# Attention worked off in pairs of units with the next sample's projections inside the drain, and a first graph layer from a 42-node operand

## What is computed

```python
# 1. tokens: 3 graph-attention layers on 4 x 128 graphs of 50 nodes, 3 -> 64 -> 128 -> 64 channels
for W, a_s, a_d, bg, R, g, b in layers:          # first layer: x has 3 channels
    h = _gat(x, src, dst, W, a_s, a_d, bg)       # softmax over the edges of a node, 4 heads
    res = x @ R
    x = gelu(_layer_norm(h + res, g, b))
h = _layer_norm(x.reshape(Bb * Tt, J * 64) @ fpW + fpb)
h = concatenate([h, text_rows_gathered_from_a_table], axis=1)      # 4 x 640 x 128
# 2. four state-space layers (scan over 640 positions, 256 channels x 64 states)
h = h + _L0_attn_ref(_layernorm(h), ...)
# 3. attention that keeps the 16 largest logits of each row, 8 heads of 16 channels
x = _layernorm(h);  x = x + depthwise_conv3(x)
q, k, v = split(x @ qkv_w.T + qkv_b)
_, idx = lax.top_k(q @ k.T * scale, 16)
out = softmax over idx, times v;  h = h + out @ wo_w.T + wo_b
```

## Time and profile before

| | |
|---|---|
| median of 3 runs | 6161.43 us (6158.26 to 6162.38) |
| the profiled execution | 6194.43 us, of which 6192.4 us are the span in the trace |
| embed_stage | 0 to about 1220 us |
| mamba_stage | about 1220 to 5400 us |
| ffn_stage | about 5400 us to the end |
| DVE busy | 5546.6 us, 90% of the span |
| PE busy | 3863.3 us, 62% |

### The profile page before, as it was taken

One profiled execution on the slowest core, in us unless ns is written; L12 is line 12 of the kernel. 1 busy time (PEld: TensorE's weight loads), 2 busy tenths in 40 slices (PEclk: granted clock), 3 DMA queues, 4 the chain that ended last, 5 costly groups with the idle time before them and its releaser, 6 DMA issues. The chain is left out here.

```text
span 6192.4 us, 60179 instructions
## 1 busy us (share of the span) xinstructions
PE 3863.3 (62%) x13720; PEld 2225.0 (36%) x13720; DVE 5546.6 (90%) x7803; ACT 3290.5 (53%) x5742; POOL 4510.6 (73%) x3041
## 2 busy tenths in 40 slices
PE   3402432237767677677676776766767766577767
PEld 3202421123334333333333333433333333265556
DVE  3798678839999999999999999999999999787778
ACT  1302232226666666666666666666666665554445
POOL 3303210329999999999999999999999999633334
PEclk9756576659999999999999999999999999888788
DMA  1000000024444444444444444444444444200000
GB/s 28 1 11 1 2 1 11 1 90 173 170 170 168 171 168 170 168 172 169 169 170 168 168 172 169 168 169 168 170 169 171 166 168 169 100 2 2 2 2 2
DMA packets 171471, 694.85 MB, mean 112 GB/s; under 512 B 27969, under 2 KB 34626, under 8 KB 171138
## 3 DMA queue, kind: packets, MB, share of 16 engines
q1 hardware_dynamic: 169608, 688.25, 30.7%
q0 software_dynamic: 1536, 3.14, 0.2%
HBM read 684.77 MB, written 6.55 MB: 112 GB/s over the span
## 5 line engine op out<-in xcount | busy, mean ns | idle before, releaser
L851 POOL TENSOR_TENSOR m_hs<-m_u,m_BC 128x1280 f32<-128x1280 f32 x1024 | 2990.4, 2920 | 76.5 <-DVE m_u L1232 76.5
L1198 DVE TENSOR_TENSOR_SCAN m_hs<-m_PS,m_hs 128x640 f32<-128x640 f32 x2048 | 2964.0, 1476 | 12.6 <-ACT m_PS L908 6.7
L1082 PE MATMUL m_PS<-m_pr,ident 128*128 128x512 f32 (+1 forms) x6144 | 2443.4, 534 | 846.5 <-DVE m_pr L1206 846.1
L1082 PEld LDWEIGHTS m_PS<-m_pr,ident 128*128 128x128 f32 x6144 | 1110.8, 191 | 2079.0 <-DVE m_pr L1206 1077.6
L908 ACT ACTIVATE m_PS<-m_dt,m_A 128x640 f32<-128x640 f32 x2048 | 1612.4, 793 | 430.5 <-DVE m_hs L1198 404.4
L858 POOL TENSOR_TENSOR m_pr<-m_hs,m_BC 128x384 f32<-128x384 f32 x1024 | 1047.5, 1023 | 95.2 <-DVE m_hs L1198 93.4
L1206 DVE TENSOR_TENSOR m_pr<-m_hs,m_PS 128x896 f32<-128x896 f32 x1024 | 1087.4, 1062 | 7.2 <-DVE m_hs L1198 6.9
L292 POOL TENSOR_TENSOR g_prod<-g_hbuf,g_E 128x128 f32<-128x128 f32 x592 | 246.1, 452 | 862.8 <-ACT g_E L344 845.6
L897 ACT COPY m_PS<-m_BC 128x448 f32<-128x448 f32 x1024 | 548.2, 535 | 427.0 <-DVE m_u L1232 83.1
L1416 POOL TENSOR_SCALAR f_negm<-f_top 128x1 f32<-128x1 f32 x160 | 33.5, 209 | 449.4 <-DVE f_top L1616 278.0
L378 PE MATMUL g_TB<-ident,g_nrm 128*128 128x128 f32 x200 | 64.3, 323 | 440.2 <-DVE g_nrm L517 429.2
(11 more groups left out here) (246 smaller groups left out, 4486.6 us busy)
## 6 DMA issues: line engine op xcount, KB each, us to landing
m_BC<-m_scr SPq DMA_DIRECT2D x1024, 640.0 KB, 3.7
m_scr<-m_CB SPq DMA_DIRECT2D x32, 160.0 KB, 4.3
m_hs<-in_cwr SPq DMA_DIRECT2D x4, 512.0 KB, 3.9
out<-f_res SPq DMA_DIRECT2D x20, 64.0 KB, 1.6
m_inw<-in_in_w SPq DMA_DIRECT2D x4, 256.0 KB, 3.9
m_dtw<-in_dw SPq DMA_DIRECT2D x4, 256.0 KB, 3.6
m_xw<-in_xw SPq DMA_DIRECT2D x8, 64.0 KB, 3.7
m_outw<-in_ow SPq DMA_DIRECT2D x4, 128.0 KB, 3.4
```

The costliest lines, as they stand in the source:

```text
L851: pool.tensor_tensor(hs[:, g % RH], u[:, p % 2], BC[:, g % UB:g % UB + 1, 0:S].to_broadcast([P, DT, S]), ALU.mult).then_inc(w_ready, 1)
L1082: ins = pe.matmul(Y[:, a:e], ident[:], pr[:, g % RP, a:e], start=False, stop=False, skip_group_check=True)
L1198: v.tensor_tensor_scan(hs[:, g % RH, d, :], half[d], hs[:, g % RH, d, :], 0.0, ALU.mult, ALU.add).then_inc(scan_done, 1)
```

## The change

Four things change.

1. **Start.** SP issues the edge loads first, then the 8 loads that the first layer needs, then the ids; it no longer waits for the clears ahead of the edge loads. The other 26 loads go out on ACT's queue. POOL makes its index rows ahead of the clears. DVE waits for the edges alone, then for the 8 first loads (the score columns of layer 0 now stand ahead of the sorted edges), and for the other 26 only ahead of layers 1 and 2.
2. **First layer.** `wc[0]` is loaded with each of its 3 rows repeated 42 times (126 rows). ACT makes 42 blocks from it, each masked to the three rows of one node (`block0`, 126 x 136 each), which live in the buffer `accB`. The coordinates of 42 nodes at a time are the stationary operand (126 rows), and one matmul of 272 columns does a group of two nodes. PE waits for all 42 blocks. For the second pair of samples the blocks are made, and the coordinates loaded, during layer 2 of the first pair.
3. **Pairs.** The attention works off units two at a time. DVE runs each of its four steps for both units before the next step; `e_all`, `negm` and `top1` have four buffers instead of two, `cut1` two instead of one. PE, ACT and POOL follow in pairs.
4. **Drain.** The loop over the samples is written out. The preparation of the next sample is cut into four steps, which stand between the last pairs of the sample before it, on every engine.

The core of the diff:

```diff
+                for dst, at in loads_first():
+                    sp.dma_start(dst, at).then_inc(first_loaded, 16)
                 sp.wait_ge(cleared, 3)
...
+                rest = loads_rest()
+                for dst, at in rest:
+                    act.dma_start(dst, at).then_inc(loaded, 16)
+                act.wait_ge(wc0_ready, 1)
+                def blocks():
+                    for j in range(CH):
+                        act.activation(block0[:, j, :], wc[0][:], ACT.Copy, scale=mask[:, j:j + 1]).then_inc(block_ready, 1)
+                blocks()
...
+                            if l == 0:
+                                k = 0 if 2 * g < CH else 1
+                                at = 2 * g - CAT[k]
+                                pe.matmul(banks(l, G).rearrange("p a n -> p (a n)"), x0C[:, bb, k, :],
+                                          block0[:, at:at + 2, :].rearrange("p a n -> p (a n)"),
+                                          start=True, stop=True).then_inc(proj_ready, 1)
...
                     if pb:
-                        sp.wait_ge(nrm_ready, pb * (3 * NG))
+                        sp.wait_ge(nrm_ready, (pb * 3 - 1) * NG)
...
-                    for c in range(UNITS + 5):
-                        if c + 1 < UNITS:
-                            logits(c + 1)
-                        if 2 <= c < UNITS + 2:
-                            transposes(c - 2)
-                        if 3 <= c < UNITS + 3:
-                            pv(c - 3)
+                    for n in range(LONG):
+                        if n >= PER + 3 and (n - PER - 3) % PER == 0:
+                            o_out((n - PER - 3) // PER, 1)
+                        old = 2 * (n - 2)
+                        if 2 <= n < PAIRS + 2:
+                            transposes(old)
+                            transposes(old + 1)
+                            pv(old)
+                        if n + 1 < PAIRS:
+                            logits(2 * n + 2)
+                            logits(2 * n + 3)
+                        if 2 <= n < PAIRS + 2:
+                            pv(old + 1)
+                        if n >= PER + 2 and (n - PER - 2) % PER == 0:
+                            o_out((n - PER - 2) // PER, 0)
+                        if b + 1 < B and 0 <= n - PAIRS < 4:
+                            prepare(b + 1, n - PAIRS)
```

More of the change, by code:

```diff
@@ L264, in _ @@
                 pool.memset(ones[:], 1.0).then_inc(iota_ready, 1)
+                pool.memset(ids[:], 4 * VOCAB).then_inc(cleared, 1)
+                pool.memset(x_tok[:], 0.0).then_inc(cleared, 1)
+                pool.memset(after[:], 0.0).then_inc(cleared, 1)
                 pool.wait_ge(cleared, 3)
@@ L433, in chain, with scores @@
                     v.wait_ge(setup, done[0])
[L435 to L438 removed]
+                def scores(l, k):
+                    n = COUT[l]
+                    for s in range(2):
+                        chain(v.tensor_tensor(awork[0:k, 0:n], wc[l][:, 0:n], avec[0:k, l, s, 0:n], ALU.mult))
+                        chain(v.tensor_reduce(wc[l][:, 2 * n + s * H:2 * n + (s + 1) * H],
+                                              awork[0:k, 0:n].rearrange("p (h c) -> p h c", h=H), AX.X, ALU.add))
+                v.wait_ge(edges_loaded, 3 * 16)
                 v.wait_ge(iota_ready, 4)
@@ L1395, in _ @@
                 pool.tensor_scalar(tap1[:], taps[:, 1:2], 1.0, None, ALU.add).then_inc(pre_pool, 1)
-                with pool.Fori(0, B) as b:
+                for b in range(B):
                     pool.wait_ge(pre_dve, b * N_DVE + 1)
@@ new lines, in prepare @@
+                def prepare(b, step):
+                    if step == 1:
+                        pe.wait_ge(pre_dve, b * N_DVE + 6)
+                        if b:
+                            pe.wait_ge(cut1_ready, b * UNITS)
+                            pe.wait_ge(exp_ready, b * UNITS)
+                        for j in range(TILES):
+                            ins = pe.transpose(LGf[:, j * P:(j + 1) * P], xn[:, j, :], ident[:])
+                        ins.then_inc(pre_pe, 1)
+                    elif step == 2:
+                        pe.wait_ge(pre_dve, b * N_DVE + 9)
+                        proj(LGf, 0, wq[:]).then_inc(pre_pe, 1)
+                        if b:
+                            pe.wait_ge(probT_copied, b * UNITS)
+                        proj(PT, 0, wk[:]).then_inc(pre_pe, 1)
+                    elif step == 3:
+                        pe.wait_ge(pre_dve, b * N_DVE + 10)
+                        for j in range(TILES):
+                            ins = pe.matmul(LGf[:, j * P:(j + 1) * P], x2[:, j * P:(j + 1) * P], wv[:],
+                                            start=True, stop=True)
+                        ins.then_inc(pre_pe, 1)
@@ L1492, in logits @@
+                for step in range(4):
+                    prepare(0, step)
+                for b in range(B):
                     def logits(c):
@@ L1592, in finish_a @@
+                for step in range(4):
+                    prepare(0, step)
+                for b in range(B):
+                    g0 = b * UNITS
                     def finish_a(t):
```

369 lines of the change are left out of this document (204 added, 165 removed).

## The result

The changed kernel takes 6057.22 us (median of 4 runs, 6031.34 to 6077.31), the kernel before 6160.3 (4 runs too). That is 103 us by the medians. The ratio is 0.9828, with a 95% interval of 0.9801 to 0.9856, which makes 106 us, or 1.7%, faster. The forecast was 6073. The profiled execution took 6077.31 us, of which 6075.6 are the span; it stands 20 above the median.

A forecast was written before the change was run, and what follows sets the result against it. Bound: TensorE at half clock in the first layer, DVE waiting for its own results in the attention. Gains 29 + 25 + 0 + 24 + 10 = 88; 6194.4 - 88 = 6106, less 33.0 (profiled execution above median): 6073; range 5965 to 6150.

The forecast's parts named there:

- start: Ahead of the first layer: TensorE starts at 48 in place of 77, a gain of 29 us.
- first pass: First layer, first two samples, during the gathers: gain counted as 0, ends a loss of 21 and a gain of 21.
- second pass: First layer, second two samples: full clock and no wait for coordinates, a gain of 25 us, 0 as other end.
- gaps between samples: Attention, last replacing to next first maximum: 31 us in place of 39.0, a gain of 3 x 8 = 24.
- pairs: Attention, two units at a time: 7.75 us a pair in place of 7.88, a gain of 10 us over 80 pairs.
- formula for T: Attention, pair time from share s at half clock: T = 1/((1 - s)/6.8 + s/12.1), 7.75 us at s = 0.28.
- B: Rival, attention: the clock holds in pairs, 6.95 us a pair at s = 0.05, total 6009 us; chance 0.25.
- C: Rival, attention: interleaving gains nothing on DVE, the pair stays at 7.88 us, total 6083 us; chance 0.04.
- D: Rival, first layer: the 126-row operand doesn't lift the clock, second pass wins only 4.5, total 6093 us; chance 0.08.
- F: Rival, start: blocks or edge loads come at the slow pace, TensorE starts at 74, total 6099 us; chance 0.08.
- E: Rival, attention: TensorE at half clock most of the time, 9.5 us a pair at s = 0.65, total 6213; chance 0.10.

The follow-up runs named there:

- three-row run: The changed kernel with 3 of the 126 rows of the first layer's stationary operand kept, so its results are not the model's: 6109.49 us (one run).
- unit-by-unit orders: The changed kernel with TensorE going transposes, logits, product for each unit: 6564.07 us; the same with ScalarE's exp ahead of its `PT` copy: 6202.67 us.

## Why the prediction was right, point by point

The time, 6057 beside a forecast of 6073, lay in the range, and the direction held. Step by step it was less good: errors cancel, and that the sum came within 16 us is luck.

| term | forecast | measured |
|---|---|---|
| start | 29 | 17.4 (45.7 against the profiled execution) |
| first pass | 0 | 20.3 |
| second pass | 25 | 27.0 |
| gaps between samples | 24 | -1.8 |
| pairs | 10 | 27.8 |
| end of the kernel | not counted | -9.6 |

The terms sum to 81 of 106. The profiled execution of the changed kernel, from which they are read, stands 20 above its median; that the other runs had a faster pattern of the attention is likely but was not profiled. Some 5 are left, about what the middle stage differs by from trace to trace.

- **Start.** The step that failed is "The chain from L458 (36.73) to TensorE's start takes 40.7 us", taken as a property of the kernel: in the two other traces of this embed_stage it takes 12.2 and 11.8. The profiled execution stood 33.0 above the median; 28 of these were that very chain's slow pace, and I used them twice, in the chain and in the 33.0 taken off at the end. L458 itself was put at 13 and came at 16.34. I forecast that the chain ends last. It ended at 27.01, and what ended last were the blocks: their 12.65 us were right (12 to 13), but they begin at 18.94, behind 26 DMA issues on the same queue and a table load.
- **First pass.** "I count 0" was the middle of two ends. Measured is the upper end, 20.3 (25.4 us of projections in place of 45.7). On the chip with the slow pace the pass took 69.2 and 69.6 us, a loss of 24, a little beyond the lower end.
- **Second pass.** Right: 23.2 us measured, 24.5 forecast, no wait, and the blocks (473 to 486) hidden in layer 2. The three-row run shows that it is the rows.
- **Gap.** "I take 31 for the gap" failed. The mechanism (transposes and projections queued behind the drain on TensorE) was named but not worked out: at half clock four units' products and transposes take until 5896.7. The sum started from the gap of before, whose drain had one or two units left, where pairs leave four. Against pairs without the drain it saves 6.7 a gap, close to the 8 that I took. The end of the kernel has the same longer drain without anything to hide it: from the last replacing 22.3 us in place of 12.8, a term that was missing.
- **Pairs.** In the fast samples (granted clock 0.94) 135.6/20 = 6.78, forecast 6.8 at full clock, and TensorE became the bound. The wait for the copy is 0.87, forecast 1.11. Slow pairs take up to 11.7, forecast 12.1. The granted clock over the samples (0.78, 0.74, 0.94, 0.94) weighted by the samples' times, is a share of 0.32 at half clock, forecast 0.28. The formula for T put 7.75, and would put 7.9 at 0.32; measured is 603.1/80 = 7.54. So the share was somewhat worse than forecast and the time better, since the formula charged too much for it. The reason given for the share was "it was in stretches without logits that the clock fell". The trace of the kernel before does not bear it out (14 of 19 falls within a sample came while logits ran), and the unit-by-unit orders speak against it. That the number was near is luck.
- **Rivals.** B (the clock holds) is what samples 3 and 4 show; C falls with the steps of 0.73; D falls; F falls as stated (TensorE starts at 31.5 to 31.9 in every trace with the new start), but on one chip the slow pace of which it speaks met the first pass. E was not the changed kernel, but an order of the same work shows what E describes: unit by unit it is 13.4 us a pair at 0.52 and 6564 us.

## What to carry to other kernels

Before a duration of a profiled execution is used, ask whether it belongs to the kernel: an execution well above the median has its surplus somewhere, and that place must be found, not subtracted at the end. Where an engine's granted clock differs between stretches of the same work, try filling its waits first; here one product moved into a wait of 0.87 us was worth 68 us, more than pairs and drain together (32 to 42). A change that moves more work behind the last input of a stage makes every drain longer, also the last, which nothing hides.

## What the runs showed of the hardware

- An operand of 3 rows left TensorE at half clock with no idle time at all; 126 rows at the same columns ran at full clock (41.98 and 23.18 us). Weight loads took 0.33 us at half clock with 3 rows and up to 0.34 with 126, and 0.19 at full clock with either. The Trainium skill, "TensorE: Matmul & The Clock Gate", section "LDWEIGHTS (loading the stationary operand)", says that a load goes by columns, not by rows; the runs agree.
- The clock read from a trace was 1.00 in the first stretch of the three-row kernel while 100 records took 45.3 us, the time of half clock.
- Two profiles of the changed kernel agree to 0.1 us in every sample, with samples of 171.9 and of 135.5 side by side, though the same instructions run in each. Its runs differ by up to 49 us (6031 to 6080).
- A dependent step of VectorE starts about 1.03 us after the one it needs, an independent one 0.73 after the one ahead of it (the earlier trace rows and the pair above), both on 640 columns.
- While 48 indirect gathers run, ACT, DVE and TensorE can start their instructions much more slowly, from 20 to 27 us after the first gather until some us after the last. It showed in the profiled execution of the kernel before and in both profiles from one chip, where the kernel before took 28 us more in all 7 runs. In the other eleven profiles the same gathers ran (17 to 83 us, or 12 to 75) and nothing was slow, so the gathers alone are not enough; the cause was not tested.
